# The rounding constant of each FP4 product tile formed on ScalarE in the slot after, instead of on VectorE in the same slot

## The reference, cut to what matters

```python
_MID = jnp.array([0.25, 0.75, 1.25, 1.75, 2.5, 3.5, 5.0], dtype=jnp.float32)

def fp4_quant_dequant(x):
    xb = x.reshape(shape[:-1] + (shape[-1] // BLOCK, BLOCK))
    scale = jnp.max(jnp.abs(xb), axis=-1, keepdims=True) / 6.0
    scale = jnp.maximum(scale, jnp.float32(1e-12))
    xn = xb / scale
    idx = jnp.searchsorted(_MID, jnp.abs(xn))
    q = _GRID[idx] * jnp.sign(xn) * scale
    return q.reshape(shape)

gate = fp4_linear(x, w_gate)
y = fp4_linear(x, w_up)
h = jax.nn.silu(gate) * y
return fp4_linear(h, w_down)
```

## Time and profile before

| | us |
|---|---|
| runs of the kernel before | 732.89 median of 3 (732.48 to 734.04) |
| the profiled execution | 728.4 |
| its span, first to last instruction | 726.6 |
| mean granted TensorE clock | 0.966 of full speed |

### The profile page before, as it was taken

One profiled execution on the slowest core, in us unless ns is written; L12 is line 12 of the kernel. 1 busy time (PEld: TensorE's weight loads), 2 busy tenths in 40 slices (PEclk: granted clock), 3 DMA queues, 4 the chain that ended last, 5 costly groups with the idle time before them and its releaser, 6 DMA issues.

```text
span 726.6 us, 10981 instructions
## 1 busy us (share of the span) xinstructions
PE 639.8 (88%) x3828; PEld 498.5 (69%) x3828; DVE 483.8 (67%) x1295; ACT 344.4 (47%) x708; POOL 227.7 (31%) x249
## 2 busy tenths in 40 slices
PE   5878899998788989988889999877889997899996
PEld 4356687877566778765677777756768784676774
DVE  5966598685777547637559685688556836766665
ACT  1144454555535464533445464444555453454553
POOL 3334555452644311005547254474310102000000
PEclk9999999999889999999999999969999999899999
DMA  8400000000000000000000000000000000001001
GB/s 270 107 1 1 1 2 1 1 1 1 1 0 1 1 1 1 1 2 1 1 0 1 1 1 1 1 1 1 1 1 1 1 1 1 1 14 30 14 24 35
DMA packets 12077, 9.63 MB, mean 13 GB/s; under 512 B 1708, under 2 KB 10744, under 8 KB 12024
## 3 DMA queue, kind: packets, MB, share of 16 engines
q1 hardware_dynamic: 12024, 8.94, 4.2%
HBM read 6.84 MB, written 2.10 MB: 12 GB/s over the span
## 4 chain that ended last, share of the span: by engine, by line
PE 69%; DVE 13%; ACT 8%; POOL 6%; issue 4%; DMA 1%; SPq 0%; ACTq 0%; POOLq 0%; DVEq 0%
PE ps L783 15%; PE ps L653 12%; PE ps L761 9%; PE ps L612 4%; PE ps L928 4%; PE ps L930 4%; PE ps L929 4%; PE ps L806 2%; PE ps L671 2%; PE ps L807 2%; PE ps L822 2%; ACT xn L1045 2%; PE ps L607 1%; PE ps L601 1%; PE ps L834 1%
## 5 line engine op out<-in xcount | busy, mean ns | idle before, releaser
L1105 ACT ACTIVATE probsT<-ps 128x512 f32<-128x512 f32 (+3 forms) x160 | 85.3, 533 | 171.3 <-PE ps L761 171.3
L783 PE MATMUL ps<-v_sb,probsT 128*128 128x129 f32 (+1 forms) x1148 | 158.1, 281 | 3.7 <-ACT probsT L1107 3.7
L783 PEld LDWEIGHTS ps<-v_sb,probsT 128*128 128x128 f32 (+1 forms) x1148 | 142.4, 192 | 10.9 <-ACT probsT L1107 5.5
L1374 DVE TENSOR_REDUCE row_max<-ps 128x1 f32<-128x512 f32 (+2 forms) x144 | 88.1, 620 | 57.9 <-PE ps L653 24.1
L761 PE MATMUL ps<-ident,probs 128*128 128x128 f32 (+1 forms) x574 | 93.9, 281 | 14.0 <-ACT hT L1035 7.1
L1079 ACT ACTIVATE probs<-ps,neg_max 128x512 f32<-128x512 f32 (+7 forms) x158 | 92.8, 618 | 12.4 <-DVE neg_max L1381 12.0
L761 PEld LDWEIGHTS ps<-ident,probs 128*128 128x128 f32 (+1 forms) x574 | 65.8, 140 | 45.5 <-issue 42.0
L511 POOL TENSOR_TENSOR hq<-ha,hp 128x352 f32<-128x352 f32 x32 | 29.9, 936 | 130.7 <-DVE hp L1417 130.7
L653 PE MATMUL ps<-k_high,q_high 128*128 128x512 f32 (+4 forms) x112 | 44.9, 401 | 3.4 <-ACT probs L1079 2.2
L1178 ACT ACTIVATE probs<-ps 128x512 f32<-128x512 f32 x40 | 24.0, 599 | 45.9 <-PE ps L930 45.9
L1609 DVE TENSOR_TENSOR probs<-probs,ps 128x512 f32<-128x512 f32 x40 | 27.4, 686 | 21.1 <-ACT probs L1178 20.5
(11 more groups left out here) (243 smaller groups left out, 1393.9 us busy)
## 6 DMA issues: line engine op xcount, KB each, us to landing
out<-x_sb SPq DMA_DIRECT2D x8, 256.0 KB, 2.3
x_sb<-in_L_attn_x SPq DMA_DIRECT2D x2, 512.0 KB, 5.9
hT_all<-in_L_wmod SPq DMA_DIRECT2D x2, 384.0 KB
rope_cos<-table_cos SPq DMA_DIRECT2D x1, 768.0 KB, 6.9
rope_sin<-table_sin SPq DMA_DIRECT2D x1, 768.0 KB, 8.1
rope_cos<-table_cos SPq DMA_DIRECT2D x1, 256.0 KB, 4.5
rope_sin<-table_sin SPq DMA_DIRECT2D x1, 256.0 KB, 6.0
moe_raw<-in_L_ffn_expert_gate_w SPq DMA_DIRECT2D x1, 256.0 KB, 3.9
```

Source lines behind the costliest of these rows:

```text
L783: mm = pe.matmul(bank(OUT_AT, 0, V_W), probsT[0:size, n % 4, k * P:(k + 1) * P], v_sb[0:size, j, :], start=(c == 0 and k == 0), stop=(c == ...
L1105: ins = act.activation(probsT[:, n % 4, 0:full], bank(TURN, 0, full), ACT.Copy)
L1374: ins = dve.tensor_reduce(dst, ps[:, start:start + width], AX.X, ALU.max, negate=single)
```

## The change

The two DVE passes on hp are taken out of the product tile's quantisation (the input groups keep them). ACT forms hp instead, as (2^9.5 ha)^2 + 12.5 * 2^19, with a Square and an Identity whose bias is a new [128, 1] constant. This `grid(n)` stands in slot n + 7 behind the slot's first two exps and ahead of everything else. POOL's `hq_scaled(n)` moves from slot n + 6 to slot n + 7, to the same place in the slot's order. PE's transposes stay at slot n + 8. DVE now raises h_scaled behind ha; ACT's tanh waits for that, not for hq_grid. The counting of DVE's steps is rewritten with the same values.

```diff
-FFN_LAG, DOWN_LAG = 6, 8
+FFN_LAG, GRID_LAG, DOWN_LAG = 6, 7, 8
...
-                    if ffn_tile(s, FFN_LAG) is not None:
-                        hq_scaled(s - FFN_LAG)
+                    if ffn_tile(s, GRID_LAG) is not None:
+                        hq_scaled(s - GRID_LAG)
...
                     act.wait_ge(gu_ready, b * TILES + n + 1)
                     if n >= 2:
-                        act.wait_ge(hq_grid, b * TILES + n - 1)
+                        act.wait_ge(h_scaled, b * TILES + n - 1)
...
+                def grid(n):
+                    act.wait_ge(h_scaled, b * TILES + n + 1)
+                    act.activation(hp[:], ha[:], ACT.Square, scale=SQUARE_SCALE).then_inc(h_squared, 1)
+                    act.wait_ge(h_squared, b * TILES + n + 1)
+                    act.activation(hp[:], hp[:], ACT.Identity, bias=square_added[:, 0:1]).then_inc(hq_grid, 1)
...
                         exp(s, 1)
+                    if ffn_tile(s, GRID_LAG) is not None:
+                        grid(s - GRID_LAG)
                     for key in input_turns(s):
...
-                    quantise(ha[:], hp[:], silu_g[:, n % 2, :], INNER // BLOCK, qh, scales_used).then_inc(hq_grid, 1)
+                    scale_blocks(ha[:], silu_g[:, n % 2, :], INNER // BLOCK, qh, scales_used).then_inc(h_scaled, 1)
```

More of the change, by code:

```diff
@@ L35 @@
 ROUND = 1.5 * 2.0 ** 22
+SQUARE_SCALE, SQUARE_ADDED = 2.0 ** 9.5, 12.5 * 2.0 ** 19
 TIES_DOWN = 1.0 - 2.0 ** -22
@@ L205, in build @@
         half = sb("half", [P, 2, GROUP])
+        square_added = sb("square_added", [P, 1])
         priority = sb("priority", [P, EXPERTS])
@@ L341, in build @@
         gu_used = sem("gu_used")
+        h_scaled = sem("h_scaled")
+        h_squared = sem("h_squared")
         hq_grid = sem("hq_grid")
@@ L453, in _ @@
             pool.memset(half[:], -0.5).then_inc(zeroed, 1)
+            pool.memset(square_added[:], SQUARE_ADDED).then_inc(zeroed, 1)
             pool.memset(ones[:], 1.0).then_inc(zeroed, 1)
@@ L458, in _ @@
                       allow_small_or_imprecise_dtypes=True).then_inc(zeroed, 1)
-            pool.wait_ge(zeroed, 10)
+            pool.wait_ge(zeroed, 11)
             pool.affine_select(out=ident[:], in_=ident[:], compare_op=ALU.not_equal, fill=1.0, base=0,
@@ L1210, in _ @@
             dve.wait_ge(setup_act, 1)
-            dve.wait_ge(zeroed, 10)
+            dve.wait_ge(zeroed, 11)
             for n in range(2 * BATCH):
@@ L1315, in _ @@
             first_maximum(-1)
-            setup_steps = steps[0]
             for b in range(BATCH):
[L1319 to L1324, removed]
                 def x_tile(t, n=1):
@@ L1400, in finish, with scale_blocks @@
                         send_statistics(0, 1 + (ffn_tile(s, DOWN_LAG) is not None), link)
-                def quantise(a, m, src, n_blocks, scales, last_wait):
+                def scale_blocks(a, src, n_blocks, scales, last_wait):
                     by_block = lambda t: t.rearrange("p (k e) -> p k e", e=BLOCK)
@@ L1411, in quantise @@
                     link(dve.reciprocal(scales[:, 1, :], scales[:, 2, :]))
-                    link(dve.scalar_tensor_tensor(
+                    return dve.scalar_tensor_tensor(
                         out=by_block(a), in0=by_block(src), scalar=TIES_DOWN,
[L1414 to L1418, removed]
+                        in1=scales[:, 1, :].unsqueeze(2).to_broadcast([P, n_blocks, BLOCK]), op0=ALU.mult, op1=ALU.mult)
                 def fp4_input(g):
@@ L1425, in fp4_input @@
                     dve.wait_ge(h_step, b * 2 * GROUPS + 2 * g + 2)
-                    quantise(qa[:], qp[:], xn[:, g, :], GROUP * P // BLOCK, qs, scales_used).then_inc(xq_grid, 1)
+                    link(scale_blocks(qa[:], xn[:, g, :], GROUP * P // BLOCK, qs, scales_used))
+                    link(dve.tensor_scalar(qp[:].bitcast(I32), qa[:].bitcast(I32), EXPONENT, None, ALU.bitwise_and))
+                    dve.tensor_scalar(qp[:], qp[:], 1.0, ROUND, ALU.max, ALU.mult).then_inc(xq_grid, 1)
                 def combine(n):
@@ L1503, in _ @@
                 take_logits(GROUPS - 1)
[L1505 to L1513, removed]
             def over_experts(t):
```

1 line of the change is left out of this document (removed).

## The result

The changed kernel took 771.55 us (median of 4 runs, 770.57 to 772.77) against 733.46 us (732.48 to 734.3) for the kernel before on the same chip: a ratio of 1.053, 95% interval 1.051 to 1.055. That is slower by 38.1 us, and 0.6 us from the forecast of 772.1. Times of runs are medians of undisturbed executions; the profiled execution of experiment 2 was a disturbed one (732.0 us, where its nine others took 719.7 to 724.5), so nothing is read from its trace.

What follows compares the result with a forecast made beforehand. PE, busy 88% of the span with 69% of the chain, was taken as the bound. Waits of 32.4 us plus 6.8 of clock gave 39.2; on the profiled 728.4 that is 767.6, plus 4.5 makes 772.1; range 750 to 791.

Steps and rivals of the forecast that it cites:

- pair on ACT: The Square and Identity added on ACT for each tile: 1.1 us together, bounds 0.93 to 1.54.
- finish(8): DVE's finish in slot 8, behind its wait for hq, starts at 111.7 instead of 108.23: +3.4 us.
- PE's transposes in slot 10: Late xq, hq and ACT's grid delay copy xqT, moving PE from 118.02 to 125.45: +7.4 us, slot 9's included.
- PE's transposes in slot 17: Late hq, ha and pair delay copies h_high and hT, moving PE from 193.90 to 199.3: +5.4 us.
- slots 16 to 18, less the xq wait: Slot 17's +5.4 us with PE's old 1.04 us wait for xq absorbed: +4.4 us.
- slots 19 to 22: Short, DVE-bound slots: hq behind shift adds 1.1 us, the pair ahead of slot 22's copies 0.9: together +2.0 us.
- The path: In and behind group slots DVE waits for POOL's hq behind modulation, ACT for DVE, PE for ACT: 16.2 us a batch.
- The clock: Half speed for 3.4 us behind the new waits at slots 10 and 13: 1.7 us each, 6.8 in all.
- The offset of 4.5 us: The median before, 732.89, lay 4.5 us above the profiled run; the same was added to the changed kernel's 767.6.
- A: Faster: DVE's wait for hq never binds and only the removal counts, 7.3 us gained, 725.6 us; chance 0.05.
- B: ACT's stand is hidden; only xq's path counts, +3.1 at slot 10, +3.0 at slot 17: 12.2, 745 us; chance 0.1.
- C: Clock stays low for 13 us instead of 3.4 after each of four new waits: 19 more, 791 us; chance 0.17.

Runs made afterwards that it cites:

- experiment 2: Kernel before without DVE's two hp passes and nothing in their place (hp a constant), hq in its old slot: 723.07 us, ratio 0.987.
- experiment 6: Changed kernel, one buffer, with ACT's pair (Square, Identity) put behind the slot's first copies instead of ahead of them: 748.43 us, ratio 1.024.
- experiment 5: Changed kernel with two buffers each of ha, hp and qh, and ACT's pair put behind the slot's first copies: 720.06 us, ratio 0.985.
- experiment 4: Changed kernel with two buffers each of ha, hp and qh, DVE waiting for the hq before the last: 730.32 us, ratio 0.998.
- experiment 1: Kernel before with only POOL's three hq passes moved a slot later, hp passes still on DVE, nothing on ACT: 761.13 us, ratio 1.040.
- experiment 10: Kernel of experiment 5 with POOL's hq also put ahead of its modulation: 723.51 us, ratio 0.989.
- experiment 3: Changed kernel with POOL's three hq passes ahead of the group's modulation instead of behind it: 756.30 us, ratio 1.033.
- experiment 8: Changed kernel with both added ACT instructions cut to one column and hp a constant, all waits and places kept: 763.08 us, ratio 1.044.
- the control with two buffers: Kernel before with two buffers of ha, hp and qh and nothing moved: 733.55 us, ratio 1.000.

## Why the prediction was right, and where its terms were off

The prediction was right in sign and in cause, and its terms, clock included, came to 39.2 us where the slots measured 42.0. That the time itself was hit to 0.6 us is luck (the offset, below). Its steps against the trace of after, batch 0, each less what had already accumulated when the step began (0.75 us at slot 8, 8.10 at slot 12, 12.18 at slot 16):

| step | forecast | measured |
|---|---|---|
| pair on ACT | 1.1 | 0.493 + 0.591 = 1.08 |
| DVE stands in slot 8 | 6 | 5.91 |
| finish(8) | +3.4 | 4.46 - 0.75 = +3.7 |
| PE's hq transposes in slot 9 | +4.4, at 113.6 | 114.55 - 0.75 = 113.8 |
| PE's transposes in slot 10 | +7.4, at 125.45 | 126.34 - 0.75 = 125.6 |
| PE's transposes in slot 13 | +2.4 | 161.24 - 150.58 - 8.10 = +2.6 |
| PE's transposes in slot 17 | +5.4 | 211.46 - 193.90 - 12.18 = +5.4 |
| slots 16 to 18, less the xq wait | +4.4 | +6.0, batch 1 +3.6 |
| slots 19 to 22 | +2.0 | +3.9, batch 1 +2.3 |
| a batch, clock included | 19.6 | 21.3 and 20.7 |

**The path** (DVE behind POOL behind the modulation, ACT behind DVE, PE behind ACT) held, and in batch 0 its steps from slot 8 to slot 17 came out to 0.3 us. PE's timeline after, at slots 13, 17 and 18:

```profile
161.24 1.09 PE L765 MATMUL ps<-ident,probs 128*128 128x128 f32 x4 [3.33 <-ACT hT L1039]
...
211.46 0.66 PE L765 MATMUL ps<-ident,probs 128*128 128x128 f32 x2 [6.41 <-ACT hT L1039]
...
223.37 0.88 PE L765 MATMUL ps<-ident,probs 128*128 128x128 f32 x3 [3.22 <-ACT xqT L1030]
```

The last one was not in the forecast. In slot 17 DVE stands 2.92 us for hq behind POOL's xq passes, as in slot 9, and in slot 18 ACT stands for ha in front of xqT, as in slot 10. The forecast walked this path for slots 9 and 10 only; for slot 18 it merely took PE's old wait for xq off the +5.4. The term came out at +6.0 for +4.4 in this batch. In batch 1 the same wait of PE was 0.85 us and the term +3.6.

**The clock** was the term that was mis-sized and misplaced. Two batches had 6.8 us of it, put behind slot 10 and slot 13. PE's windows after (us, length, busy, granted clock):

```profile
126.00:130.00 4.00, 3.62 (x20) 1.00 0.00 0
160.00:164.00 4.00, 2.77 (x8) 0.62 0.01 2
...
222.00:232.00 10.00, 7.66 (x24) 0.52 0.00 0
430.00:438.00 8.00, 6.24 (x20) 0.57 0.00 1
```

Behind slot 10 of batch 0 it stayed at 1.00; in batch 1 the same place ran at half speed (the mean is 0.57 from 430 to 438), behind a wait of 2.59 us for 1.64, and slots 8 to 11 cost 9.8 us there for 7.35 in batch 0. Behind slot 13 it fell as forecast. Behind slot 18 it fell for the whole 10 us, where the forecast saw no new cost. PE was busy 13.3 us longer on the same work, about twice the clock term, and idle 30.2 us longer where the slot terms say 32.4. Part of the 13.3 lies in the set-up, where the granted clock from 34 to 44 was 0.53 after and 1.00 before. So the clock's share was sized at about half and the waits slightly high; together the span grew by 43.5 for 39.2.

**The offset of 4.5 us** was added in the belief that the median of the changed kernel lies as far above its profiled run as before. It doesn't: its profiled run took 771.9 us and its median is 771.55. What filled the place of the 4.5 is 2.8 us more in the slots (42.0 for 39.2) and some 1.6 in stretches that have no FFN in them (0.75 ahead of slot 8, 0.9 between the batches). Two errors of like size and opposite sign make the hit. The last section shows where the 4.5 comes from.

**Rivals.** A (faster) needed hq ahead of DVE; the trace has POOL's L507 at 106.21 and hq behind it. Its price of 7.3 us lies between the two readings of experiment 2 (10.3 by the medians, 5.8 against the short executions), so it is not shown to be off. B (ACT's stand hidden) is refuted by PE's 27.0 us in front of hT. Yet 745 is close to what experiment 6 measured, 748.4, in a kernel where that stand is away from the copies. The working was less good than this looks: it had 12.2 us, all at slots 10 and 17, and by the slots that kernel lost 19.4 (9.4 and 10.1), 5.9 of them in slots 8 to 11 of batch 0, where B had 3.1. C (clock low for 13 us behind each new wait) did not come: the new stretches are some 4 to 10 us long. Only behind slot 16 of batch 1 did the new stretch join with the one that was there before, to 17 us in all.

**Contention.** Before, hp's first pass took 1.30 us in slot 8, beside POOL's modulation; its mean of 0.463 mixes 28 passes of 0.34 us with 4 of 1.3. The GPSIMD Engine Reference of the Trainium skill (Specifications) says that GpSimd and VectorE share their SBUF interfaces, with contention for DVE instructions in a 2-port mode or with two SBUF inputs. The longer passes beside POOL's agree with it; which mode the passes ran in, no run here shows. By that rule alone the change gains (rival A), and without the passes, with hq where it was, experiment 2 is faster indeed. The delay was real; it wasn't what sets the end of the changed kernel.

## What to carry to other kernels

When work is moved one step later in a pipeline, list every buffer that it still reads and ask who writes it next: with single buffers the move can close a ring of waits, and the stand is then set by what is queued ahead of the moved work on its engine, here a modulation and three FP4 passes, not by the work itself alone. Give the ring a second buffer first (here worth 41 us), and then place the added instructions behind the copies that PE waits for: 1.07 us ahead of one such copy cost 3.5 here. To find out which of several stands matters, repair one at a time and see whether the gains add.

## What the runs showed of the hardware

**The clock can amplify a short wait.** In slot 13 a PE wait of 1.03 us (experiment 5) left the granted clock at 1.00, and one of 2.04 us at the same place (experiment 4) was followed by some 6 us at half speed. The first costs nothing more; the second cost 2.5 us on top of its own extra length. The length of the wait alone doesn't decide it. In the traces read here the wait for hT in slot 13 was 1.01 to 1.04 us in sixteen cases (two batches of eight kernels), and three of them were followed by half speed: both batches of experiment 1 and the first of experiment 10. All eight waits of 2.04 to 3.33 us there (after, experiments 3, 4 and 8) were followed by a lower clock. PE in slot 13 of experiment 1, and its window:

```profile
156.92 1.08 PE L761 MATMUL ps<-ident,probs 128*128 128x128 f32 x4 [1.02 <-ACT hT L1035]
```

```profile
156.00:160.00 4.00, 3.08 (x8) 0.58 0.01 4
```

In slot 10 of the kernel after, a wait of 1.64 us left the clock alone (batch 0), while in batch 1 one of 2.59 us was followed by half speed.

**Two times for one program.** Of 19 runs of the kernel before beside experiments 1 to 4, five took 728.6 to 728.9 us and the others 732.8 to 734.9, with nothing between. Its profiled run is one of the quick ones; the profiled run of the control with two buffers, whose slots are as long to within 1.0 us a batch, is one of the others. PE's windows in the set-up and between the batches, before and then in the control (us, length, busy of PE, PEld, DVE, ACT, POOL, granted clock):

```profile
34.00:44.00 10.00, 6.71 (x46) 4.83 (x44) 7.08 (x19) 5.32 (x15) 0.00 (x0) 1.00 0.01 2
322.00:332.00 10.00, 8.65 (x45) 5.55 (x45) 6.69 (x23) 3.17 (x11) 3.63 (x4) 1.00 0.00 1
```

```profile
34.00:44.00 10.00, 8.59 (x32) 6.58 (x33) 4.80 (x14) 3.58 (x8) 0.00 (x0) 0.55 0.01 2
322.00:332.00 10.00, 8.49 (x32) 5.26 (x30) 3.31 (x11) 2.01 (x5) 0.00 (x0) 0.66 0.00 1
```

The same instructions got half speed in one run and full speed in the other. What decides it stays open. It means that a difference between medians can be off by some 5 us, and the slots tell more: by these the kernel of experiment 5 is 8.6 us quicker than before (4.2 and 4.4 a batch), while the medians say 13.3; against the short executions of the kernel before (728.3 to 728.8 in that comparison) its 720.06 is some 8.5 quicker too. By the slots the two-buffer kernel of experiment 4 equals the kernel before (+0.6 and +0.4 us).

**ScalarE's price.** Square on 352 columns took 0.493 us, Identity with a pointer 0.591; on one column 0.197 and 0.294. ScalarE: Activation LUTs of the Trainium skill (What ACT_TABLE_LOAD costs) has a fixed cost, a cost per column and an addition for a pointer; estimates worked out from them are 0.479, 0.572, 0.187 and 0.280. The trace agrees to 3 to 5%, and lies above each.
